# Four passes of an attention tile moved within their engines' order

## The chip, the cores and the metric

The kernel runs on one core of a Trainium2 chip, as one program. The metric is the device time of one execution in microseconds (us), shown as the median of several runs. The engines are TensorE (PE, with its weight loads as PEld), VectorE (DVE), ScalarE (ACT), GpSimd (POOL) and SyncE (SP), which here only issues DMAs. Each engine works through its own instructions in the order in which they are written; they meet at semaphores.

## The reference, cut to what matters

Four layers follow one another on x of 8 x 1024 x 256 in float32: an attention layer, an fp8 linear layer, a Mamba mixer with its MLP, and an int8 gated MLP. The change is in the first one alone:

```
q = (x @ Wq.T + bq);  k = (x @ Wk.T + bk);  v = (x @ Wv.T + bv)      # 16 heads of 16
logits = li[:, :, None, :] + lj[:, None, :, :] + rel_b               # 3 relations per pair of tokens
relation_probs = softmax(logits, axis=-1)
bias = einsum('bijk,hk->bhij', relation_probs, logical_bias)
gate = sigmoid(x @ gate_W.T + gate_b)
attn_weights = softmax(q k / scale + gate * bias, axis=-1)           # over j, for each head
out = einsum('bhij,bjhd->bihd', attn_weights, v) @ Wo.T + bo
```

x is layer-normed before it and added to the result.

## The kernel before

`attention` walks over 64 tiles of 128 rows of queries (8 batches of 8 tiles). The order of every engine is written out by hand: each has a function `body`, called once for each tile t, which loops over the 16 heads (`for u in range(H)`) and puts the other work of the tile between the heads by an `if` on u. `run` calls the bodies, the middle 48 tiles in a hardware loop. Flags say what a tile has: `look` (a next tile whose relation is prepared; 63 tiles), `pro` (projections for a tile one batch ahead; 56 tiles) and `post` (a previous tile to finish).

For head u of tile t the work runs through four engines:

- `pe_s`: TensorE makes the scores in `ps_s`, 128 x 1024 (L647). There is one such buffer, so head u+1 waits for DVE's `dve_s` of head u.
- `dve_f` (L491) on DVE writes rho * ps_p + R, the head's bias, into one of 8 row buffers (`srow`), for 12 heads. For the heads 1, 4, 8 and 12 (`POOL_HEADS`) `pool_f` does it on POOL in two passes, a multiplication (L408) and an addition (L410). `dve_f` of head u+1 stands ahead of `dve_s` of head u.
- `dve_s` (L502) on DVE takes the scores, adds the gated bias and finds the row's extremum (`nmax`), in one pass of 1024.
- `act_e` (L576) on ACT is the exponential in place; `pe_t` (L658) turns the row in eight blocks into `ps_t`, two heads later; `act_at` (L585) copies them out; `pe_pv` (L670) multiplies with V.

The relation of the next tile (64 x 128 x 1024 numbers each for three relations) is prepared in the same loop, by this chain:

- `dve_rel` step 0 (L474) on DVE: RT = max(Dj + a, 0), one tensor input and a scalar for each partition, both in SBUF. Step 1 (L477): a second maximum, with two tensor inputs in SBUF.
- `pool_rel` (L382), two passes on POOL, behind `pool_rem` (L372), which belongs to the projections and waits for `act_hi` (L542) on ACT.
- `act_rel` (L557, L561), three exponentials on ACT.
- `pool_sum` (L387, L391) on POOL.
- `act_y0` on ACT: a logarithm (step 0, L568), then an exponential of its negative (step 1, L571), which is the reciprocal of the sum.
- `pool_t` (L395) on POOL, `dve_y` (L482) on DVE, `pool_p` (L400) on POOL, and `act_p` (L537), which puts the probabilities into `ps_p` for the next tile's `dve_f`.

The other passes that the change or the prediction speaks of: `dve_v` (L455 and L459) adds V's bias from `ps_m`, which TensorE's `pe_v` filled (L635); `dve_xn` (L440) applies the layer norm of a later tile, one tensor input in SBUF; `act_o` (L589) copies the output of the tile before from `ps_o`, `pe_oT` (L680) turns it, and `dve_norm` (L508, L510) divides it; `pool_xrb` (L427) adds the output's bias. `ps_m` is one bank that the projections and the output of the tile before use in turn, under the semaphores `pm_free` and `om_free`.

POOL's order in a tile is: f of head 4, `pool_rem`, `pool_rel` twice, rstd, `pool_lo`, f of head 8, `pool_sum` twice, f of head 12, `pool_xrb`, `pool_t`, `pool_ge`, `pool_p` twice, `pool_gT`, f of the next tile's head 1, `pool_kappa`. The change doesn't touch it.

Of the kernel before, what the change touches and what calls it, by code (L numbers as in the profile page):

```python
# [34 lines left out]
def wait(eng, sem, value):  # L35

    if isinstance(value, int) and value <= 0:
        return
    eng.wait_ge(sem, value)
# [10 lines left out]
def attention(nc, x_in, wqk, wvg, bqk, rows, ident_in, parts_d, x_out):  # L50
# [13 lines left out]
    with ExitStack() as ctx:  # L64
# [365 lines left out]
        def dve_ln(dve, p, k):  # L430
            wait(dve, x_in_s, 16 * p + 16)
            nc.vector.bn_stats(stats[:], xt[:, k, :]).then_inc(ln_step, 1)
            alone(dve, ln_step, 3 * p + 1, dve_own)
            nc.vector.bn_aggr(mv[:], stats[:]).then_inc(ln_step, 1)
            dve.wait_ge(ln_step, 3 * p + 2)
            nc.vector.tensor_scalar(ve[:], mv[:, 1:2], LN_EPS, None, ALU.add).then_inc(ln_step, 1)
# [28 lines left out]
        def dve_rel(dve, t, k, slot, step):  # L465

            d10, d20 = (Dj[:, i, S * (slot // NT):S * (slot // NT) + S] for i in range(2))
            a10, a20 = (small[:, slot, H + i:H + i + 1] for i in range(2))
            if step == 0:
                wait(dve, kap_ok, t + 1)  # L470
                wait(dve, a12_ok, t + 1)
                wait(dve, p_ok, 2 * t)
                wait(dve, pm_free, 4 * (t - slot % NT + NT) - 1)
                nc.vector.tensor_scalar(RT[:], d10, a10, 0.0, ALU.add, ALU.max).then_inc(rel_step, 1)  # L474
            elif step == 1:
                dve.wait_ge(rel_step, 2 * t + 1)
                nc.vector.scalar_tensor_tensor(RT[:], d20, a20, RT[:], ALU.add, ALU.max).then_inc(rel_step, 1)  # L477
# [6 lines left out]
        def dve_f(dve, t, k, h):  # L484
            if h in POOL_HEADS:
                return
            r = rows_sb[h % NROW]
            if h == 0:
                wait(dve, pc_ok, t + 1)
            wait(dve, t_ok, 2 * (H * t + h) + 2)  # L490
            nc.vector.scalar_tensor_tensor(r[:], ps_p[:], rho[:, h:h + 1], R[k][0][:],  # L491
                                           ALU.mult, ALU.add).then_inc(fd_ok, 1)
# [61 lines left out]
        def act_rel(act, t, k, slot, step):  # L554
            if step == 0:
                wait(act, rel_step, 2 * t + 2)
                nc.scalar.activation(R[k][0][:], RT[:], ACT.Exp, scale=-1.0).then_inc(rel_exp, 1)  # L557
            else:
                wait(act, rel_d, 2 * t + step)
                dst = (R[k][1], R2)[step - 1]  # L560
                nc.scalar.activation(dst[:], dst[:], ACT.Exp,  # L561
                                     bias=small[:, slot, H + step - 1:H + step]).then_inc(rel_exp, 1)

        def act_y0(act, t, step):

            if step == 0:
                wait(act, rel_sum, 2 * t + 2)
                nc.scalar.activation(R2[:], RT[:], ACT.Ln).then_inc(rel_y0, 1)  # L568
            else:
                act.wait_ge(rel_y0, 2 * t + 1)  # L570
                nc.scalar.activation(R2[:], R2[:], ACT.Exp, scale=-1.0).then_inc(rel_y0, 1)  # L571

        def act_e(act, t, h):
            wait(act, s_ok, H * t + h + 1)
            r = rows_sb[h % NROW]
            nc.scalar.activation(r[:], r[:], ACT.Exp, scale=-1.0, bias=nmax[:, h % NROW:h % NROW + 1]  # L576
                                 ).then_inc(e_ok, 1)
# [9 lines left out]
        def act_o(act, o):  # L587
            wait(act, pv_ok, 2 + HG * (o + 1))
            nc.scalar.copy(O4[:], ps_o[:]).then_inc(o_ok, 1)  # L589
# [166 lines left out]
        def after(par, ib, n):  # L756

            return (par * NT + ib + n) % (2 * NT)
# [141 lines left out]
        def _(dve):  # L900
# [49 lines left out]
                dve_f(dve, 0, 0, 0)  # L950

            def body(dve, t, k, par, ib, pro, post, look, before):
                for u in range(H):
                    if u + 1 < H:
                        dve_f(dve, t, k, u + 1)
                    dve_s(dve, t, k, after(par, ib, 0), u)
                    if look and u < 2:
                        dve_rel(dve, t + 1, 1 - k, after(par, ib, 1), u)
                    if pro and u == 2:
                        dve_ln(dve, t + AHEAD, 1 - k)  # L960
                    if u == 3 and (not isinstance(t, int) or t >= 2):
                        dve_out(dve, t - 2)
                    if pro and u == 5:
                        dve_xn(dve, t + AHEAD, 1 - k)
                    if pro and u == 4:
                        dve_v(dve, t + NT, 1 - par, ib)
                    if post and u == 6:
                        dve_norm(dve, t - 1)
                    if look and u == 10:
                        dve_y(dve, t + 1)  # L970
                    if pro and u == 13:
                        dve_gate(dve, t + NT)
                    if pro and u == 14:
                        dve_qk(dve, t + AHEAD)
                    if look and u == 15:
                        dve_f(dve, t + 1, 1 - k, 0)
# [68 lines left out]
        @block.scalar  # L1045
        def _(act):
            def start(act):
                act.wait_ge(w_ready, 1)
                act_g_t(act, 0)
                act_xT(act, NT)  # L1050
                act_g_d(act, 0)
                act_g_e(act, 0)
                act_d(act, NT, NT)
                for s in range(2):
                    act_g_hi(act, 0, s)
                act_g_t(act, 1)
                for s in range(2):
                    act_g_mid(act, 0, s)
                act_g_ge(act, 0)
                act_g_d(act, 1)  # L1060
                act_g_e(act, 1)
                act_rel(act, 0, 0, 0, 0)
                act_rel(act, 0, 0, 0, 1)
                act_rel(act, 0, 0, 0, 2)
                for s in range(2):
                    act_g_hi(act, 1, s)
                for s in range(2):
                    act_g_mid(act, 1, s)
                for step in range(2):
                    act_y0(act, 0, step)  # L1070
                act_p(act, 0, 0)
                act_hi(act, NT)
                act_g_ge(act, 1)
                act_mid(act, NT)
                act.wait_ge(g_st, 16 * 8)

            def body(act, t, k, par, ib, pro, post, look, before):
                for u in range(H):
                    act_e(act, t, u)
                    if post and u == 5:  # L1080
                        act_o(act, t - 1)
                    if pro and u == 7:
                        act_xT(act, t + AHEAD)
                    if look and u in (7, 8):
                        act_y0(act, t + 1, u - 7)
                    if u >= LAG:
                        act_at(act, t, u - LAG)
                    elif post:
                        act_at(act, t - 1, H + u - LAG)
                    if u == 0 and (not isinstance(t, int) or t >= 2):  # L1090
                        act_aT(act, t - 2)
                    if followed(t, pro) and u == 0:
                        act_hi(act, t - 1 + AHEAD)
                    if followed(t, pro) and u == 2:
                        act_mid(act, t - 1 + AHEAD)
                    if look and u in (1, 3, 4):
                        act_rel(act, t + 1, 1 - k, after(par, ib, 1), (1, 3, 4).index(u))
                    if pro and u == 6:
                        act_gate(act, t + NT, 1 - par, ib)
                    if pro and u == 10:  # L1100
                        act_d(act, t + AHEAD, after(par, ib, AHEAD))
                    if look and u == 13:
                        act_p(act, t + 1, 1 - k)

            def finish(act):
                for u in range(H - LAG, H):
                    act_at(act, TILES - 1, u)
                act_aT(act, TILES - 2)
                act_o(act, TILES - 1)
                act_aT(act, TILES - 1)  # L1110

            act.preload_act_table_set("natural_log_exp_and_others")
            act.sem_inc(at_ok, 2)
            run(act, start, body, finish)

        @block.tensor
# [1296 lines left out]
```

## Time and profile before

| | us |
|---|---|
| median of 3 runs | 6053.53 (6041.44 to 6056.1) |
| the profiled execution, its own time | 6048.23 |
| its span | 6046.4 |
| attention, from 100 to 2830 us of the span | 2730.00, of which DVE is busy 2567.55, ACT 2623.23, PE 2409.03, POOL 2250.26 |

The span is the time between the first and the last instruction of the profiled execution. Busy times are sums over an engine's instructions. A tile's period is the distance between the starts of the same instruction in two tiles that follow one another. Durations overlap a little at their ends: the next instruction of DVE usually starts 0.08 us before the printed end of the one ahead.

### The profile page before, as it was taken

The numbers are of one execution on the slowest core, as the hardware profiler recorded it, in microseconds if no ns is written. First come the engines' busy times: TensorE is split into PE (matmuls) and PEld (weight loads), VectorE is DVE, ScalarE is ACT, GpSimd is POOL, SyncE is SP. The second block draws the span as 40 slices with busy tenths as digits, with TensorE's granted clock in tenths as the row PEclk, the third lists the DMA queues.
The fourth block names the chain that finished last, engine by engine and source line by source line (L and its number), as shares of the span: only waits on it lengthen the run. The fifth ranks groups of instructions, "written<-read, shape, count | busy, mean of one in ns | idle before, by whom it ended". The sixth has DMA issues, their size and how long they took to land. (4 is left out here: it accounts for less than half of the span.)

```text
span 6046.4 us, 122850 instructions
## 1 busy us (share of the span) xinstructions
PE 5371.3 (89%) x40162; PEld 3536.9 (58%) x40162; DVE 4703.6 (78%) x6099; ACT 4404.3 (73%) x7005; POOL 3700.2 (61%) x2010
## 2 busy tenths in 40 slices
PE   6888888888888898888799869999999979999999
PEld 4666666666666666655344345555555546666665
DVE  6999999999999999998898679999999942122221
ACT  4999999999999999999366678888888821111111
POOL 3888888888888888775100069999999930000000
PEclk8999999999999999999899889999999989999999
DMA  2121121212112121200355555565555531111110
GB/s 76 26 50 30 28 52 28 52 28 51 28 35 45 31 49 31 44 19 13 123 197 213 185 211 185 210 207 189 197 202 209 180 106 40 47 35 35 35 35 11
DMA packets 461360, 538.76 MB, mean 89 GB/s; under 512 B 237536, under 2 KB 337760, under 8 KB 460784
## 3 DMA queue, kind: packets, MB, share of 16 engines
q1 hardware_dynamic: 460784, 531.75, 28.1%
q8 instruction: 279, 4.57, 0.3%
q14 instruction: 297, 2.43, 0.1%
HBM read 370.31 MB, written 161.35 MB: 88 GB/s over the span
## 5 line engine op out<-in xcount | busy, mean ns | idle before, releaser
L502 DVE CUSTOM_DVE_ANT_0 srow<-srow,ps_s,small 128x1024 f32<-128x1024 f32 x1024 | 1305.0, 1274 | 71.6 <-issue 49.8
L576 ACT ACTIVATE srow<-srow,nmax 128x1024 f32<-128x1024 f32 x1024 | 1199.7, 1172 | 94.8 <-DVE nmax L502 83.0
L585 ACT COPY AT<-ps_t 128x512 f32<-128x512 f32 x2048 | 1110.6, 604 | 24.2 <-PE ps_t L658 23.4
L658 PEld LDWEIGHTS ps_t<-ident,srow 128*128 128x128 f32 x8192 | 959.2, 141 | 222.6 <-issue 16.8
L658 PE MATMUL ps_t<-ident,srow 128*128 128x128 f32 x8192 | 1077.1, 274 | 2.8 <-ACT AT L585 2.4
L1977 POOL TENSOR_TENSOR c_hc<-c_hs,c_cs 128x1024 f32<-128x1024 f32 x432 | 1010.1, 2365 | 63.9 <-DVE c_hs L2079 62.1
L491 DVE SCALAR_TENSOR_TENSOR srow<-ps_p,rho,R 128x1024 f32<-128x1024 f32 x768 | 976.0, 1271 | 0.0
L1938 PE MATMUL c_ps_y<-c_hc,c_ident 128*128 128x512 f32 x2048 | 945.9, 595 | 30.0 <-POOL c_hc L1977 17.1
L2079 DVE TENSOR_TENSOR_SCAN c_hs<-c_da,c_pd 128x1024 f32<-128x1024 f32 x384 | 859.8, 2274 | 58.0 <-PE c_pd L1929 54.6
L647 PE MATMUL ps_s<-K,Q 96*128 96x512 bf16 x2048 | 621.3, 385 | 286.8 <-DVE nmax L502 271.5
L2022 ACT ACTIVATE c_sT<-c_dxT,c_bT 128x256 f32<-128x256 f32 x1536 | 668.4, 494 | 105.7 <-PE c_pd L1929 95.7
L410 POOL TENSOR_TENSOR srow<-srow,R 128x1024 f32<-128x1024 f32 x256 | 608.1, 2376 | 46.9 <-POOL srow L408 46.9
L670 PE MATMUL ps_o<-AT,V 128*32 128x128 f32 x16384 | 609.6, 278 | 0.0
L2215 POOL TENSOR_TENSOR d_rstd<-d_ve,d_mhalf 128x4 f32<-128x4 f32 x16 | 16.3, 1017 | 899.1 <-DVE d_ve L1222 899.1
L1938 PEld LDWEIGHTS c_ps_y<-c_hc,c_ident 128*128 128x128 f32 x2048 | 359.9, 191 | 345.5 <-issue 304.7
L1929 PEld LDWEIGHTS c_pd<-c_ident,c_sT 128*128 128x128 f32 x3072 | 354.1, 142 | 343.0 <-issue 199.3
L1929 PE MATMUL c_pd<-c_ident,c_sT 128*128 128x128 f32 x3072 | 407.8, 276 | 109.5 <-DVE c_hc L2086 81.1
L670 PEld LDWEIGHTS ps_o<-AT,V 128*32 128x32 f32 x16384 | 402.9, 110 | 130.3 <-issue 128.6
L2013 ACT ACTIVATE c_da<-c_dt,c_a_neg 128x1024 f32<-128x1024 f32 x384 | 435.8, 1135 | 5.0 <-issue 5.0
L647 PEld LDWEIGHTS ps_s<-K,Q 96*128 96x128 bf16 x2048 | 141.6, 98 | 475.4 <-DVE nmax L502 420.9
L1970 POOL TENSOR_TENSOR c_db<-c_dx,c_bs 128x1024 f32<-128x1024 f32 x128 | 302.1, 2361 | 122.7 <-DMA c_bs<-bc_d 122.7
L2242 DVE TENSOR_TENSOR d_x<-d_ps_y,d_y 128x512 f32<-128x512 f32 x32 | 22.1, 692 | 438.6 <-PE d_ps_y L2317 438.6
(256 smaller groups left out, 8571.8 us busy)
## 6 DMA issues: line engine op xcount, KB each, us to landing
c_cs<-bc_d SPq DMA_DIRECT2D x256, 512.0 KB, 4.2
c_bs<-bc_d SPq DMA_DIRECT2D x64, 512.0 KB, 6.6
Q<-parts_d SPq DMA_DIRECT2D x384, 64.0 KB, 2.2
parts_d<-parts SPq DMA_DIRECT2D x57, 384.0 KB, 3.3
K<-parts_d SPq DMA_DIRECT2D x168, 128.0 KB, 4.3
sz_d<-b_sz SPq DMA_DIRECT2D x16, 1024.0 KB, 7.2
xv_d<-b_xv SPq DMA_DIRECT2D x16, 1024.0 KB, 7.9
dt_d<-b_ab SPq DMA_DIRECT2D x16, 1024.0 KB, 4.2
```

The source lines that it names most:

```text
L491: nc.vector.scalar_tensor_tensor(r[:], ps_p[:], rho[:, h:h + 1], R[k][0][:], ALU.mult, ALU.add).then_inc(fd_ok, 1)
L502: nc.vector.tensor_tensor_reduce(r[:], r[:], ps_s[:], small[:, slot, h:h + 1], BIG, ALU.add, ALU.min, nmax[:, h % NROW:h % NROW + 1]).then ...
L576: nc.scalar.activation(r[:], r[:], ACT.Exp, scale=-1.0, bias=nmax[:, h % NROW:h % NROW + 1]).then_inc(e_ok, 1)
L585: nc.scalar.copy(AT[h % NAT][:, HG * half:HG * half + HG, :], ps_t[:, half]).then_inc(at_ok, 1)
L647: last = nc.tensor.matmul(ps_s[:, n * 512:(n + 1) * 512], Q6[k][:, h, :], K6[:, h, n * 512:(n + 1) * 512], start=True, stop=True)
L658: last = nc.tensor.transpose(ps_t[:, half, i, :], rows_sb[h % NROW][:, j * P:(j + 1) * P], ident[:])
L670: last = nc.tensor.matmul(ps_o[32 * i:32 * i + 32, j, :], V[par][:, n, h, :], AT[h % NAT][:, n, :], start=(n == 0), stop=(n == NT - 1))
L1929: last = nc.tensor.transpose(pd[:, c, k * P:(k + 1) * P], src[:, k, c * P:(c + 1) * P], ident[:])
L1938: last = nc.tensor.matmul(ps_y[:, c, cut], ident[:], hc[place((n, c)) % NHC][:, cut], start=n == 0, stop=n == NS - 1)
L1977: nc.gpsimd.tensor_tensor(hc[place((n, c)) % NHC][:], hs[place((n, c)) % NHS][:], cs[n % NCS][:], ALU.mult).then_inc(hp_ok, 1)
L2022: last = nc.scalar.activation(sT[i % NSC][:, k, :], dxT[p][:, k, :], ACT.Copy, scale=bT[p][:, k, n:n + 1])
L2079: nc.vector.tensor_tensor_scan(h, gain, push, 0.0, ALU.mult, ALU.add).then_inc(h_ok, 1)
```

## The change

Four passes are written at other places. On DVE, `dve_rel` step 0 goes from behind `dve_s` of head 0 to the front of the tile, where it stands between `dve_f` of head 0 (which the body of the tile before issues last) and `dve_s` of head 0; and `dve_v` goes from behind `dve_s` of head 4 to behind `dve_xn`, which is behind `dve_s` of head 5. On ACT, `act_y0` step 1 goes from behind `act_e` of head 8 to ahead of it, and `act_o` from behind `act_e` of head 5 to ahead of it. No pass is added, removed or altered, and the orders of PE, POOL and SP stay.

```diff
@@ DVE's body @@
             def body(dve, t, k, par, ib, pro, post, look, before):
+                if look:
+                    dve_rel(dve, t + 1, 1 - k, after(par, ib, 1), 0)
                 for u in range(H):
                     if u + 1 < H:
                         dve_f(dve, t, k, u + 1)
                     dve_s(dve, t, k, after(par, ib, 0), u)
-                    if look and u < 2:
-                        dve_rel(dve, t + 1, 1 - k, after(par, ib, 1), u)
+                    if look and u == 1:
+                        dve_rel(dve, t + 1, 1 - k, after(par, ib, 1), 1)
                     if pro and u == 2:
                         dve_ln(dve, t + AHEAD, 1 - k)
                     if u == 3 and (not isinstance(t, int) or t >= 2):
                         dve_out(dve, t - 2)
                     if pro and u == 5:
                         dve_xn(dve, t + AHEAD, 1 - k)
-                    if pro and u == 4:
+                    if pro and u == 5:
                         dve_v(dve, t + NT, 1 - par, ib)
@@ ACT's body @@
                 for u in range(H):
+                    if look and u == 8:
+                        act_y0(act, t + 1, 1)
                     act_e(act, t, u)
-                    if post and u == 5:
-                        act_o(act, t - 1)
                     if pro and u == 7:
                         act_xT(act, t + AHEAD)
-                    if look and u in (7, 8):
-                        act_y0(act, t + 1, u - 7)
+                    if look and u == 7:
+                        act_y0(act, t + 1, 0)
                     if u >= LAG:
                         act_at(act, t, u - LAG)
...
                     if look and u in (1, 3, 4):
                         act_rel(act, t + 1, 1 - k, after(par, ib, 1), (1, 3, 4).index(u))
+                    if post and u == 4:
+                        act_o(act, t - 1)
```

What stands in DVE's order at the seam between two tiles (L447 and L449 finish the queries and keys of a tile ahead; the L491 is head 0's, the second L502 pair head 0's), before:

```order
140 L447 SCALAR_TENSOR_TENSOR qkf<-ps_m,b_qk,eT 128x128 x2
141 L449 TENSOR_TENSOR qkf<-ps_m,b_qk 128x256
142 L502 ISA srow,nmax<-srow,ps_s,small 128x1024
143 L502 ISA nmax 128x1
144 L491 SCALAR_TENSOR_TENSOR srow<-ps_p,rho,R_0 128x1024
145 L502 ISA srow,nmax<-srow,ps_s,small 128x1024
146 L502 ISA nmax 128x1
147 L474 TENSOR_SCALAR RT<-Dj,small 128x1024
148 L491 SCALAR_TENSOR_TENSOR srow<-ps_p,rho,R_0 128x1024
```

And now:

```order
140 L447 SCALAR_TENSOR_TENSOR qkf<-ps_m,b_qk,eT 128x128 x2
141 L449 TENSOR_TENSOR qkf<-ps_m,b_qk 128x256
142 L502 ISA srow,nmax<-srow,ps_s,small 128x1024
143 L502 ISA nmax 128x1
144 L491 SCALAR_TENSOR_TENSOR srow<-ps_p,rho,R_0 128x1024
145 L474 TENSOR_SCALAR RT<-Dj,small 128x1024
146 L502 ISA srow,nmax<-srow,ps_s,small 128x1024
147 L502 ISA nmax 128x1
148 L491 SCALAR_TENSOR_TENSOR srow<-ps_p,rho,R_0 128x1024
```

The relation pass L474 has moved one pass of L502 forward, to right behind head 0's L491.

DVE's order around heads 4 to 6 (the first L502 is head 4's), before:

```order
105 L502 ISA srow,nmax<-srow,ps_s,small 128x1024
106 L502 ISA nmax 128x1
107 L455 TENSOR_TENSOR V<-ps_m,row 128x16x16
108 L459 TENSOR_TENSOR zg<-ps_m,b_misc 128x18
109 L491 SCALAR_TENSOR_TENSOR srow<-ps_p,rho,R_0 128x1024
110 L502 ISA srow,nmax<-srow,ps_s,small 128x1024
111 L502 ISA nmax 128x1
112 L440 TENSOR_SCALAR xn<-xt,mv,rstd 128x256
113 L491 SCALAR_TENSOR_TENSOR srow<-ps_p,rho,R_0 128x1024
```

And now:

```order
105 L502 ISA srow,nmax<-srow,ps_s,small 128x1024
106 L502 ISA nmax 128x1
107 L491 SCALAR_TENSOR_TENSOR srow<-ps_p,rho,R_0 128x1024
108 L502 ISA srow,nmax<-srow,ps_s,small 128x1024
109 L502 ISA nmax 128x1
110 L440 TENSOR_SCALAR xn<-xt,mv,rstd 128x256
111 L455 TENSOR_TENSOR V<-ps_m,row 128x16x16
112 L459 TENSOR_TENSOR zg<-ps_m,b_misc 128x18
113 L491 SCALAR_TENSOR_TENSOR srow<-ps_p,rho,R_0 128x1024
```

V's two passes have moved from ahead of head 6's L491 to behind the layer norm's L440.

## Rows read from the trace of the kernel before

**Rows 1.** Busy time by stretch: start:end, length, then busy us of each engine

```profile
100.00:2830.00 2730.00, 2409.03 (x28884) 1803.76 (x28883) 2567.55 (x3700) 2623.23 (x3971) 2250.26 (x1342) 0.99 0.16 36
```

**Rows 2.** DVE's timeline, a tile's head: start, duration, engine, line, [idle before <-releaser]

```profile
1525.24 1.28 DVE L491 SCALAR_TENSOR_TENSOR srow<-ps_p,rho,R 128x1024 f32<-128x1024 f32 x1
1526.80 1.28 DVE L502 CUSTOM_DVE_ANT_0 srow<-srow,ps_s,small 128x1024 f32<-128x1024 f32 x1 [0.28 <-DVE srow L491]
...
1528.00 0.90 DVE L474 TENSOR_SCALAR RT<-Dj,small 128x1024 f32<-128x1024 f32 x1
1528.82 1.27 DVE L491 SCALAR_TENSOR_TENSOR srow<-ps_p,rho,R 128x1024 f32<-128x1024 f32 x1
...
1531.21 1.27 DVE L477 SCALAR_TENSOR_TENSOR RT<-Dj,small,RT 128x1024 f32<-128x1024 f32 x1
...
1568.39 1.28 DVE L491 SCALAR_TENSOR_TENSOR srow<-ps_p,rho,R 128x1024 f32<-128x1024 f32 x1
```

**Rows 3.** POOL's timeline, the same tile

```profile
1524.67 1.12 POOL L408 TENSOR_SCALAR srow<-R,rho 128x1024 f32<-128x1024 f32 x1 [0.55 <-PE ps_t L658]
1525.98 2.37 POOL L410 TENSOR_TENSOR srow<-srow,R 128x1024 f32<-128x1024 f32 x1 [0.18 <-POOL srow L408]
```

**Rows 4.** DVE's timeline, the kernel's first tile

```profile
89.54 1.54 DVE L474 TENSOR_SCALAR RT<-Dj,small 128x1024 f32<-128x1024 f32 x1
...
93.39 2.29 DVE L477 SCALAR_TENSOR_TENSOR RT<-Dj,small,RT 128x1024 f32<-128x1024 f32 x1
```

**Rows 5.** POOL's timeline, the kernel's first tile

```profile
88.18 2.35 POOL L410 TENSOR_TENSOR srow<-srow,R 128x1024 f32<-128x1024 f32 x1 [0.18 <-POOL srow L408]
90.50 1.56 POOL L408 TENSOR_SCALAR srow<-R,rho 128x1024 f32<-128x1024 f32 x1
92.24 2.36 POOL L410 TENSOR_TENSOR srow<-srow,R 128x1024 f32<-128x1024 f32 x1 [0.18 <-POOL srow L408]
```

**Rows 6.** Lines L474 and L440 over attention: duration ns min/median/max

```profile
L474 DVE TENSOR_SCALAR RT<-Dj,small x63: 817/899/1537, 89.5 to 2783.9; 128x1024 f32<-128x1024 f32 x63
...
L440 DVE TENSOR_SCALAR xn<-xt,mv,rstd x56: 409/567/2093, 107.7 to 2499.8; 128x256 f32<-128x256 f32 x56
```

**Rows 7.** POOL's timeline, the rest of that tile

```profile
1531.27 2.24 POOL L372 TENSOR_TENSOR qkf<-qkf,parts 128x512 f32<-128x512 f32 x1 [2.91 <-ACT parts L542]
...
1541.10 2.38 POOL L410 TENSOR_TENSOR srow<-srow,R 128x1024 f32<-128x1024 f32 x1 [0.18 <-POOL srow L408]
...
1552.22 0.75 POOL L427 TENSOR_TENSOR xr<-xr,row 128x256 f32<-128x256 f32 x1
1553.84 2.39 POOL L395 TENSOR_TENSOR RT<-RT,R 128x1024 f32<-128x1024 f32 x1 [0.87 <-ACT R L571]
```

**Rows 8.** DVE's timeline, behind head 4 to head 10 of that tile

```profile
1540.27 0.42 DVE L455 TENSOR_TENSOR V<-ps_m,row 128x256 f32<-128x256 f32 x1 [0.33 <-PE ps_m L635]
...
1540.69 1.27 DVE L491 SCALAR_TENSOR_TENSOR srow<-ps_p,rho,R 128x1024 f32<-128x1024 f32 x1
...
1543.08 0.56 DVE L440 TENSOR_SCALAR xn<-xt,mv,rstd 128x256 f32<-128x256 f32 x1
1543.56 1.27 DVE L491 SCALAR_TENSOR_TENSOR srow<-ps_p,rho,R 128x1024 f32<-128x1024 f32 x1
...
1556.26 1.23 DVE L482 SCALAR_TENSOR_TENSOR R<-RT,R 128x1024 f32<-128x1024 f32 x1 [0.46 <-POOL RT L395]
```

**Rows 9.** ACT's timeline, the reciprocal's exponential in that tile

```profile
1551.53 1.19 ACT L576 ACTIVATE srow<-srow,nmax 128x1024 f32<-128x1024 f32 x1
1552.58 1.08 ACT L571 ACTIVATE R<-R 128x1024 f32<-128x1024 f32 x1
```

**Rows 10.** TensorE's timeline, scores of head 12 of that tile

```profile
1558.74 0.60 PE L647 MATMUL ps_s<-K,Q 96*128 96x512 bf16 x2 [0.41 <-DVE nmax L502]
```

**Rows 11.** DVE's timeline, a tile of the last batch (no projections)

```profile
2675.61 0.26 DVE L508 RECIPROCAL rinv<-ps_m 128x16 f32<-128x16 f32 x1 [1.13 <-PE ps_m L680]
...
2685.38 1.23 DVE L482 SCALAR_TENSOR_TENSOR R<-RT,R 128x1024 f32<-128x1024 f32 x1 [0.67 <-POOL RT L395]
```

## The prediction

> **What bounds the kernel now.** I read the stretches first, since the change is in attention alone. From 100 to 2830 us of the span DVE is busy 2567.55 of 2730.00 us (94%) and ACT 2623.23 (96%) [rows 1]. Both are close to full, so a microsecond that DVE or ACT loses in a tile is a microsecond of the kernel unless a wait further on takes it up. Then I read the timelines of one tile in the middle, and follow its starts. Head 0's L491 starts at 1525.24 and that of the next tile at 1568.39, a period of 43.15 us [rows 2]. DVE's idle pieces in it are small, and each has a cause of its own: 0.28 us ahead of head 0's L502, which waits for the result of the L491 right ahead of it [rows 2]; 0.33 for TensorE ahead of V's bias, and 0.46 for POOL's L395 ahead of L482 [rows 8]. Taken one by one the moves aim at these.
>
> The third view decides, and it is POOL's timeline laid beside DVE's. L474 has one tensor input and 1024 columns, and is printed with 0.90 us, shorter than L491's 1.27 with as many columns. It starts at 1528.00 and ends at 1528.90 [rows 2]. POOL's addition for head 4 started at 1525.98 and ends at 1528.35 [rows 3], 0.55 ahead. In the first tile L474 starts at 89.54 and takes 1.54, to 91.08 [rows 4]; POOL's addition runs from 88.18 to 90.53 [rows 5], again 0.55 ahead. So L474's own work is 0.55 us, and the rest of its printed time is spent until POOL's pass is over: one starts 0.35 us ahead of POOL's end, the other 0.99, and both end 0.55 behind it. The same holds elsewhere: L440 starts at 1543.08 and ends at 1543.64 [rows 8], 0.16 behind the end of POOL's second pass for head 8 (1541.10 + 2.38 = 1543.48) [rows 7], and can take 0.41 or 2.09 [rows 6]; L477, with two inputs in SBUF, takes 1.27 alone [rows 2], but 2.29, to 95.68, when it comes into a POOL pass that ends at 94.60 [rows 4, 5]. It goes the other way too. POOL's L408 takes 1.12 [rows 3] but 1.56 where L474 holds on until 91.08 [rows 4, 5], and L372, half as wide as the passes of 2.38, takes 2.24, because L477 runs until 1532.48 [rows 2, 7]. These passes of DVE and those of POOL exclude one another. L491 and L502, which take one input from PSUM, run through POOL's passes at their usual length [rows 2, 3].
>
> The Trainium skill says this in SBUF — State Buffer, section "SBUF: two separate sides": VectorE and GpSimd share a pair of ports, whoever starts first holds it for its whole instruction, and the other is blocked. It counts VectorE's two-port modes and instructions with two SBUF inputs among the holders. By that rule the relation pass can't be put into GpSimd's addition at its printed price, which speaks against this change; the sum by the rule is the one below.
>
> **The change part by part.** All numbers are shifts of starts against the tile above.
>
> *The relation pass at the front.* Head 0's L491 starts at 1525.24 and lasts 1.28; the next instruction of DVE can start 0.08 ahead of its end, at 1526.44. There L474 now stands. POOL's addition has held on since 1525.98 and does until 1528.35 [rows 3], so L474 ends at 1528.90, as it did before, after 2.46 us in place of 0.90. Head 0's L502 then starts at 1528.82 in place of 1526.80, and head 2's L491 one pass of L502 (1.20) later, at 1530.02 in place of 1528.82 [rows 2]: +1.20 us. The 0.28 us of idle time is gone, and is counted in this. Without the exclusion L474 would give the place at once and everything from here would come 0.36 earlier.
>
> What could hide the 1.20? Queued behind L474 on DVE are all heads. ACT has e of head 0 later by 2.02, but catches up over its pieces of waiting by head 2. POOL's next pass, L372, waits for ACT's L542 and after that ends about 1.03 behind L477 [rows 2, 7]. L477 comes 1.20 later, L372 ends 1.20 later, and all of POOL's line up to head 8 with it.
>
> *V's bias behind the layer norm.* V's two passes take 0.42 from 1540.27 to 1540.69, and the wait ahead of them is 0.33, or 0.41 counted from start to start [rows 8]. Both leave this place: 1.20 - 0.83 = +0.37 when L440 comes up, at 1543.45. But POOL's pass for head 8 now ends at 1543.48 + 1.20 = 1544.68 [rows 7], and L440 0.16 behind it, at 1544.84. What V's passes filled before is now spent inside L440. They follow from 1544.76, and head 7's L491 starts at 1545.18 in place of 1543.56 [rows 8]: +1.62. TensorE's `pe_oT` waits for V in `pm_free`, and head 7's scores stand behind it; but these wait for head 6's L502, which follows head 7's L491 and so V itself by over 1.2 us. V's later place costs TensorE nothing.
>
> *The output copy ahead of head 5's exponential.* ACT does the same work; the exponential of head 5 comes one copy later, and its row is transposed two heads further on. DVE's `dve_norm` stands behind head 6, and head 7's scores wait for head 6 anyway. Nothing here; it is worth something only in the last batch, below.
>
> *The reciprocal's exponential ahead of head 8's.* L571 stood one exponential later than it will, 1552.58 against 1551.53 [rows 9], and POOL's L395 waited 0.87 for it [rows 7]. POOL is free for L395 at 1552.22 + 0.75 = 1552.97 before, 1554.17 now. ACT's exponential of head 6 waits for DVE, so ACT is as late as DVE here, about 1.65: L571 starts at 1551.53 + 1.65 and ends at about 1554.3, and L395 at 1556.7. L482 comes up on DVE at 1556.26 - 0.54 + 1.62 = 1557.34 [rows 8], and waits no more. The 0.54 (0.46 of idle and 0.08 of overlap) are given back: +1.08.
>
> *Behind it.* TensorE had 0.41 us of room ahead of head 12's scores [rows 10]; it is 1.62 late against DVE's 1.08, so 0.13 of the difference stays. The tile ends between +1.08 and +1.21; I take +1.2. POOL's first pass for head 4 waits for TensorE's transposes of head 12 [rows 3] and is as late as DVE is, so the next tile meets the same addition at the same place.
>
> *Tiles.* 56 tiles have projections. In the first of them L474 would come at about 88.0, ahead of the addition at 88.18 [rows 5], and is spared. 55 x 1.2 = 66 us. In the 7 further tiles with a relation pass but no projections the +1.20 meets a wait of 1.13 for `pe_oT` [rows 11], which the earlier output copy takes away, and 0.67 for L395; I count 0. Bounds for each of the 55: without V's loss in L440, +1.20 - 0.83 + 0.42 = +0.79 ahead of L482, and +0.3 to +0.4 behind it; with no wait given back at L482, +1.62.
>
> **The sum.** 6048.23 + 66 = 6114 for the profiled execution. Its time lies 5.3 us below the median of 6053.53, whose runs span 15 us, so the median would be 6120; I take the middle, 6117. Under 0.3% (18 us) this kernel's measurement doesn't tell from no change.
>
> **The rivals.**
> *L474 gets in first* (ends on the other side). If it comes up before 1525.98, it takes 0.55 and POOL's addition waits, as L408 did in the first tile. Then head 0's L502 starts at 1526.96, head 2's L491 0.66 early, L477 and POOL too. L440 keeps DVE back until 0.16 behind the head 8 pass, V's 0.42 follow, -0.24; L482 waits for nothing, -0.78; TensorE's line gives about -0.65. 55 x -0.65 = -36: 6015. Speaks for it: the margin is only 0.46 (1526.44 against 1525.98). Against: the addition is tied to head 12's transposes, these to the same scores as DVE's passes, and to reverse the order takes the whole margin in every tile. Chance 0.08.
> *No exclusion at the new place at all*, whatever makes L474 end 0.55 behind POOL now: L474 would cost 0.82, head 2 would come 0.36 early, and POOL's chain from L542 to L395 would let the tile gain 0.44: 55 x -0.44 = -24, 6027. Sixty-three of sixty-three starts speak against it in that none is shorter than 0.817 us. Chance 0.03.
> *V isn't caught in L440*: only the lower bound, 55 x 0.35 = 19, 6070. It needs POOL's head 8 pass to be less late than DVE. POOL sits idle 2.91 us ahead of L372 [rows 7], which speaks for it; that L477 now and then decides when L372 can work speaks against. Chance 0.13.
> *ACT or TensorE falls behind for good*, so that the wait at L482 isn't given back: 55 x 1.62 = 89, 6140. ACT at 96% speaks for it. Chance 0.10.
> *Nothing moves the end*, as DVE's loss meets slack that I don't see: 6050. Chance 0.03.
> The forecast itself (6100 to 6133) has 0.63.
>
> **How the numbers follow.** The time is the forecast's. The range leaves out both gains and no change (0.14) and reaches from the lower to the upper bound: 6066 to 6142. Faster by over 0.3%: 0.11. Slower by over 0.3%: the forecast, the upper case and most of the lower one, 0.84. The rest, 0.05.
>
> **What would show it.** In the changed kernel's trace L474 should take about 2.4 us nearly everywhere and end 0.55 behind a POOL L410; L440 should take about 1.4; V's wait for TensorE and that of L482 for L395 should be gone; ACT should wait about 2 us for head 0's `nmax`; the period should be 44.3. L474 at 0.55 to 0.9 us would prove me wrong, and so would L440 at 0.57 with a period near 43.5.

## The result, and the profile after

The changed kernel takes 6134.04 us (median of 4 runs, 6126.8 to 6151.94) against 6054.32 before: a ratio of 1.0146, 95% interval 1.0129 to 1.0163. By the ratio that is some 88 us slower; the two medians are 80 us apart. Some executions were disturbed (a granted clock of 0.37 to 0.93, three of e8's six among them), and every number here is of undisturbed ones.

The profiled execution took 6132.81 us, 85 more than the one before, and nearly all of that is in attention. From the first L477 to the last it was 2694 us and is 2777, by DVE's timelines (93.39 to 2787.46 before, 94.16 to 2871.61 after).

DVE's timeline of a tile in the middle, to be laid beside [rows 2] and [rows 8] (start, duration, engine, line):

```profile
1714.44 1.28 DVE L491 SCALAR_TENSOR_TENSOR srow<-ps_p,rho,R 128x1024 f32<-128x1024 f32 x1
1715.64 2.46 DVE L474 TENSOR_SCALAR RT<-Dj,small 128x1024 f32<-128x1024 f32 x1
1718.02 1.27 DVE L502 CUSTOM_DVE_ANT_0 srow<-srow,ps_s,small 128x1024 f32<-128x1024 f32 x1
...
1721.61 1.27 DVE L477 SCALAR_TENSOR_TENSOR RT<-Dj,small,RT 128x1024 f32<-128x1024 f32 x1
...
1732.64 1.40 DVE L440 TENSOR_SCALAR xn<-xt,mv,rstd 128x256 f32<-128x256 f32 x1
1733.96 0.41 DVE L455 TENSOR_TENSOR V<-ps_m,row 128x256 f32<-128x256 f32 x1
...
1746.54 1.22 DVE L482 SCALAR_TENSOR_TENSOR R<-RT,R 128x1024 f32<-128x1024 f32 x1
...
1758.72 1.28 DVE L491 SCALAR_TENSOR_TENSOR srow<-ps_p,rho,R 128x1024 f32<-128x1024 f32 x1
```

POOL's timeline of the same tile, to be laid beside [rows 3, 7]:

```profile
1715.18 2.37 POOL L410 TENSOR_TENSOR srow<-srow,R 128x1024 f32<-128x1024 f32 x1 [0.18 <-POOL srow L408]
1722.47 1.44 POOL L372 TENSOR_TENSOR qkf<-qkf,parts 128x512 f32<-128x512 f32 x1 [4.93 <-ACT parts L542]
...
1731.51 2.38 POOL L410 TENSOR_TENSOR srow<-srow,R 128x1024 f32<-128x1024 f32 x1 [0.18 <-POOL srow L408]
...
1743.62 2.38 POOL L395 TENSOR_TENSOR RT<-RT,R 128x1024 f32<-128x1024 f32 x1 [0.28 <-ACT R L571]
```

L474 comes up at 1715.64, 0.46 us into POOL's addition, which ends at 1717.55; L474 ends 0.55 later, at 1718.10. L440 ends at 1734.04, 0.15 behind POOL's pass for head 8 (1733.89). The waits ahead of V's L455 and ahead of L482 are gone. From L491 to L491 it is 44.28 us, against 43.15.

In the first tile the two meet in the other order. L474 starts at 89.75 and takes 0.74, to 90.49; POOL's addition starts 0.14 behind it and takes 2.80 in place of 2.37:

```profile
89.89 2.80 POOL L410 TENSOR_TENSOR srow<-srow,R 128x1024 f32<-128x1024 f32 x1 [0.18 <-POOL srow L408]
```

The lines L474 and L440 over the whole of attention (ns, min/median/max):

```profile
L474 DVE TENSOR_SCALAR RT<-Dj,small x63: 737/2454/2722, 89.7 to 2865.2; 128x1024 f32<-128x1024 f32 x63
...
L440 DVE TENSOR_SCALAR xn<-xt,mv,rstd x56: 1327/1416/2183, 107.3 to 2576.5; 128x256 f32<-128x256 f32 x56
```

Two tiles by stretch (start:end, length, busy us of PE, PEld, DVE, ACT and POOL, then TensorE's granted clock as a share of full speed, the DMA engines' busy share and GB/s):

```profile
1721.61:1765.89 44.28, 38.40 (x474) 29.07 (x464) 43.03 (x61) 41.71 (x65) 35.70 (x22) 1.00 0.12 29
1541.66:1587.68 46.02, 41.66 (x456) 31.30 (x448) 43.22 (x63) 41.34 (x64) 35.59 (x22) 0.91 0.19 38
```

The first is what was forecast. The second was not: 46.02 us at a mean granted clock of 0.91. Of the 62 periods from L477 to L477, 18 take more than 45 us, against 6 before. TensorE's timeline in the second tile:

```profile
1539.40 0.60 PE L647 MATMUL ps_s<-K,Q 96*128 96x512 bf16 x2 [2.57 <-DVE nmax L502]
...
1555.86 0.63 PE L680 MATMUL ps_m<-ident,O 128*128 128x128 f32 x4 [1.07 <-ACT O L589]
1557.03 0.60 PE L647 MATMUL ps_s<-K,Q 96*128 96x512 bf16 x2 [0.55 <-DVE nmax L502]
1557.48 1.76 PE L658 MATMUL ps_t<-ident,srow 128*128 128x128 f32 x8
1559.17 1.51 PE L670 MATMUL ps_o<-AT,V 128*32 128x128 f32 x24
...
1561.51 1.04 PE L658 MATMUL ps_t<-ident,srow 128*128 128x128 f32 x8
```

The same tile's stretches around its two waits, in the columns of the windows above:

```profile
1538.00:1540.50 2.50, 1.10 (x8) 0.91 (x9) 2.50 (x5) 1.12 (x2) 0.00 (x0) 1.00 1.00 152
1540.50:1544.00 3.50, 3.50 (x40) 2.22 (x39) 3.50 (x5) 2.99 (x6) 1.35 (x2) 0.51 1.24 166
1557.50:1561.00 3.50, 3.50 (x35) 2.70 (x34) 2.59 (x4) 3.36 (x7) 2.97 (x3) 0.52 0.02 7
```

TensorE waits 2.57 us for head 0's `nmax`, then runs a stretch at 0.51, which is the lower of its two levels, 1.2 GHz. It waits again ahead of the turned output (1.07) and of head 7's scores (0.55), and again runs at half: eight transposes take 1.76 us instead of 1.04, and 24 products 1.51 instead of the 0.86 of the tile at full clock. The DMA engines move much in the first of the two slow stretches (a busy share printed as 1.24) and next to nothing in the second (0.02), so DMA traffic isn't what they share. Head 8's scores come late, and DVE has 1.53 us of idle time ahead of its L502 of head 8, where the tile at full clock has none:

```profile
1561.85 1.28 DVE L502 CUSTOM_DVE_ANT_0 srow<-srow,ps_s,small 128x1024 f32<-128x1024 f32 x1 [1.53 <-issue]
```

The Trainium skill, TensorE: Matmul & The Clock Gate, Part 1, says that a monitor sets this clock by how busy the engine has been recently; the rows agree in that both drops stand behind waits.

### The profile page after: what moved, and what is told of

Its sections match the earlier page's. It is cut to its first block and busy times, and to the rows that moved or that the text cites. A ratio compares the mean times of both kernels' runs of the same rounds, so it can differ in the third digit from the quotient of the medians.

```text
span 6131.0 us, 122850 instructions
## 1 busy us (share of the span) xinstructions
PE 5412.3 (88%) x40162; PEld 3566.3 (58%) x40162; DVE 4823.9 (79%) x6099; ACT 4390.8 (72%) x7005; POOL 3658.4 (60%) x2010
## 5 line engine op out<-in xcount | busy, mean ns | idle before, releaser
L502 DVE CUSTOM_DVE_ANT_0 srow<-srow,ps_s,small 128x1024 f32<-128x1024 f32 x1024 | 1304.1, 1274 | 90.6 <-issue 66.4
L658 PEld LDWEIGHTS ps_t<-ident,srow 128*128 128x128 f32 x8192 | 974.8, 143 | 250.3 <-ACT AT L585 34.7
L658 PE MATMUL ps_t<-ident,srow 128*128 128x128 f32 x8192 | 1098.0, 278 | 13.1 <-ACT AT L585 12.7
L491 DVE SCALAR_TENSOR_TENSOR srow<-ps_p,rho,R 128x1024 f32<-128x1024 f32 x768 | 975.5, 1270 | 0.0
L647 PE MATMUL ps_s<-K,Q 96*128 96x512 bf16 x2048 | 633.6, 391 | 329.1 <-DVE nmax L502 313.6
L670 PE MATMUL ps_o<-AT,V 128*32 128x128 f32 x16384 | 628.3, 284 | 0.0
L670 PEld LDWEIGHTS ps_o<-AT,V 128*32 128x32 f32 x16384 | 415.2, 112 | 136.3 <-issue 133.7
```

Source lines behind the costliest of these rows:

```text
L502: nc.vector.tensor_tensor_reduce(r[:], r[:], ps_s[:], small[:, slot, h:h + 1], BIG, ALU.add, ALU.min, nmax[:, h % NROW:h % NROW + 1]).then ...
L647: last = nc.tensor.matmul(ps_s[:, n * 512:(n + 1) * 512], Q6[k][:, h, :], K6[:, h, n * 512:(n + 1) * 512], start=True, stop=True)
L658: last = nc.tensor.transpose(ps_t[:, half, i, :], rows_sb[h % NROW][:, j * P:(j + 1) * P], ident[:])
L670: last = nc.tensor.matmul(ps_o[32 * i:32 * i + 32, j, :], V[par][:, n, h, :], AT[h % NAT][:, n, :], start=(n == 0), stop=(n == NT - 1))
```

## The experiments

Ratios, and the times given with a sign, are to the kernel before, run on the same chip in turn. The periods are the distances between the starts of `dve_rel`'s step 1 in DVE's timeline, 62 of them. The period "at full clock" is the median of those whose granted clock stays at 1.00; "below full clock" are those with a lower mean.

### One part of the change at a time

e1, the relation pass alone (a diff against before):

```diff
+                if look:
+                    dve_rel(dve, t + 1, 1 - k, after(par, ib, 1), 0)
                 for u in range(H):
...
-                    if look and u < 2:
-                        dve_rel(dve, t + 1, 1 - k, after(par, ib, 1), u)
+                    if look and u == 1:
+                        dve_rel(dve, t + 1, 1 - k, after(par, ib, 1), 1)
```

> The first relation pass alone moved to the tile's front; V and the two ACT passes where they were. Exclusion theory (a DVE pass of L474's kind waits until POOL's running pass is over): L474 takes about 2.45 us and ends 0.55 behind POOL's addition for head 4, head 2 comes 1.20 late, and since POOL's whole line follows L477, the wait ahead of L482 stays: period about 44.3 us, and the time about as much above before as the whole change (+65 to +90 us). Rival theory (the price is V's pass caught behind L440, and L474 is cheap because the 0.28 us of idle time ahead of it goes): period 43.15 or less, time within 20 us of before.

Measured: 1.0163 (1.0139 to 1.0187), +98 us, more than the whole change and more than the +65 to +90 expected. L474 has a median of 2453 ns. At full clock the period is 44.35; other tiles take 45.3 and 46.8. The exclusion theory holds for the tile, and the rival falls. The excess lies in the 35 periods below full clock; e10 tests whether the clock makes it.

e2, V's bias alone:

```diff
-                    if pro and u == 4:
+                    if pro and u == 5:
                         dve_v(dve, t + NT, 1 - par, ib)
```

> V's bias alone moved behind the layer norm's L440. Exclusion theory: V's wait of 0.33 us goes, L440 comes 0.83 us earlier but still ends 0.16 us behind POOL's pass for head 8, so it takes about 1.4 us, head 7 comes 0.42 late, and the wait ahead of L482 shrinks from 0.46 to about 0 in exchange: period 43.15, time within 10 us of before. Rival theory (the waits of DVE are independent prices): the 0.33 us is gained in each of 55 tiles, -18 us. Second rival (V behind L440 is the change's price): +20 us or more.

Measured: 1.0100 (1.0080 to 1.0120), +60 us. That is in the range of the second rival, +20 us or more, and V behind L440 does have a price: the period at full clock is 43.56, not 43.15. But 0.41 us in 56 tiles are only 23 us. The rest lies in the 38 periods below full clock, most of them of 44.6 to 44.9 us. DVE's timeline of a tile at full clock:

```profile
1222.24 1.39 DVE L440 TENSOR_SCALAR xn<-xt,mv,rstd 128x256 f32<-128x256 f32 x1
1223.55 0.41 DVE L455 TENSOR_TENSOR V<-ps_m,row 128x256 f32<-128x256 f32 x1
...
1227.29 1.28 DVE L502 CUSTOM_DVE_ANT_0 srow<-srow,ps_s,small 128x1024 f32<-128x1024 f32 x1 [0.22 <-PE ps_s L647]
...
1236.66 1.23 DVE L482 SCALAR_TENSOR_TENSOR R<-RT,R 128x1024 f32<-128x1024 f32 x1 [0.45 <-POOL RT L395]
```

L440 takes 1.39 as expected, but the wait ahead of L482 is still 0.45. ACT's exponential of head 6 waits for DVE (0.28 us), so the reciprocal and with it L395 come as late as DVE does, and the 0.42 of V's passes can't go into that wait.

TensorE shows the other half. Its waits ahead of head 6's scores and of the turned output, first in the kernel before (the tile of [rows 8]), then in e2's tile above, where the second line is the wait ahead of head 7's scores:

```profile
1543.22 0.61 PE L647 MATMUL ps_s<-K,Q 96*128 96x512 bf16 x2 [0.67 <-DVE nmax L502]
1545.48 0.63 PE L680 MATMUL ps_m<-ident,O 128*128 128x128 f32 x4 [0.78 <-ACT O L589]
```

```profile
1225.47 0.63 PE L680 MATMUL ps_m<-ident,O 128*128 128x128 f32 x4 [1.52 <-ACT O L589]
1226.49 0.60 PE L647 MATMUL ps_s<-K,Q 96*128 96x512 bf16 x2 [0.39 <-DVE nmax L502]
```

With V out of the way head 6's scores no longer wait, but the turned output comes no earlier. Two waits of 0.67 and 0.78 us have become one of 1.52 and one of 0.39.

e3, the two ACT passes alone, which is the second half of the change's diff:

```diff
+                    if look and u == 8:
+                        act_y0(act, t + 1, 1)
                     act_e(act, t, u)
-                    if post and u == 5:
-                        act_o(act, t - 1)
...
+                    if post and u == 4:
+                        act_o(act, t - 1)
```

> The two ACT passes alone moved (output copy ahead of head 5's exponential, reciprocal's exponential ahead of head 8's), DVE as before. My working: POOL's L395 starts 0.87 us earlier, the wait of 0.46 ahead of L482 goes, TensorE's line limits the gain to about 0.41 us a tile: period 42.7, time -20 to -28 us. Rival (ACT is at 96% and its order doesn't matter, the wait comes back as another): period 43.1, time within 8 us of before.

Measured: 0.9960 (0.9944 to 0.9977), -24 us, with a period of 42.67. Both are as worked out.

e4, all but the relation pass: e2's and e3's diffs together.

> The whole change without the first relation pass: V's bias and both ACT passes moved. Exclusion theory: V's pass behind L440 costs 0.42 us, the earlier L395 gives back 0.54: period 43.0 to 43.15, time -10 to 0 us against before; so the relation pass alone makes the change's loss. Rival (V behind L440 is the price): +20 us or more.

Measured: 1.0059 (1.0041 to 1.0076), +36 us. At full clock the period is 43.08, inside what was expected. The time is not: -10 to 0 us was expected, and +36 is in the rival's range. 38 of the 62 periods are below full clock, many of them of 44.6 us. Against e3 the V move costs 0.41 us a tile at full clock and about 60 us in all.

At full clock the three parts add up: 1.20 for the relation pass (e1), 0.41 for V (e2) and -0.48 for ACT's passes (e3) make 1.13 us a tile, and the change has 1.14. The whole times don't: 98 + 60 - 24 = 134 us, and the change has 88.

### The exclusion, from both sides

e5, POOL's addition for head 4 left out (head 4's bias lacks the term R, and the semaphore is counted up at once):

```diff
-            nc.gpsimd.tensor_tensor(r[:], r[:], R[k][0][:], ALU.add).then_inc(fp_ok, 1)
+            if h == 4:
+                pool.sem_inc(fp_ok, 1)
+            else:
+                nc.gpsimd.tensor_tensor(r[:], r[:], R[k][0][:], ALU.add).then_inc(fp_ok, 1)
```

> The whole change, and POOL's addition for head 4 (the second of its two passes, the one that runs while the relation pass comes up) left out, so that head 4's bias lacks one term; its semaphore is counted up at once. Exclusion theory: L474 takes 0.55 us at the new place instead of 2.45, head 2 comes about 0.66 us early, and the period of a tile in which TensorE's clock stays up is 42.5 us. Rival theory (L474 is slow at its new place because of what stands next to it on DVE or because of its operands): it stays at 2.4 us, the period at 44.3. The stalls of TensorE ahead of the turned output stay, so some tiles still lose about 1.5 us to the lower clock: time -36 to +5 us against before.

Measured: 0.9944 (0.9929 to 0.9958), -34 us. The moved pass, which is L477 in this kernel, over all of attention (ns, min/median/max):

```profile
L477 DVE TENSOR_SCALAR RT<-Dj,small x63: 737/743/754, 89.6 to 2759.5; 128x1024 f32<-128x1024 f32 x63
```

The instruction, its operands and its place are those of the change; only POOL's pass is gone, and 2454 ns become 743. The period at full clock is 42.59, against 42.5 expected. The pass's own work is 0.74 us, not 0.55.

e6, the maximum taken with a tensor in PSUM in place of zero (from the second tile on, so another result):

```diff
-                nc.vector.tensor_scalar(RT[:], d10, a10, 0.0, ALU.add, ALU.max).then_inc(rel_step, 1)
+                if isinstance(t, int) and t == 0:
+                    nc.vector.tensor_scalar(RT[:], d10, a10, 0.0, ALU.add, ALU.max).then_inc(rel_step, 1)
+                else:
+                    nc.vector.scalar_tensor_tensor(RT[:], d10, a10, ps_p[:], ALU.add, ALU.max).then_inc(rel_step, 1)
```

> The whole change, but the moved relation pass takes the maximum with ps_p, a tensor in PSUM, in place of zero (one input in SBUF, one in PSUM, as L491; it computes something else from the second tile on). Exclusion theory: like L491 it runs through POOL's passes and takes 1.27 us at the new place, about 1.1 us less than in the change though it needs more than twice the 0.55 us for itself; period at full clock about 43.05 us, as with all but the relation pass moved, time +25 to +45 us against before. Rival theory (the pass is slow at the front of the tile whatever it reads): 2.4 us again, period 44.3.

Measured: 1.0054 (1.0040 to 1.0069), +33 us. DVE's timeline, then POOL's, in this kernel:

```profile
1511.62 1.27 DVE L477 SCALAR_TENSOR_TENSOR RT<-Dj,small,ps_p 128x1024 f32<-128x1024 f32 x1
1512.81 1.28 DVE L505 CUSTOM_DVE_ANT_0 srow<-srow,ps_s,small 128x1024 f32<-128x1024 f32 x1
```

```profile
1511.17 2.38 POOL L410 TENSOR_TENSOR srow<-srow,R 128x1024 f32<-128x1024 f32 x1 [0.18 <-POOL srow L408]
```

It comes up 0.45 us into POOL's addition, as in the change, and ends 0.66 us before it, after 1.27 us. An instruction that needs 0.74 us alone was made one that needs 1.27, and a tile at full clock became 1.2 us shorter (43.1). So the place alone doesn't make the pass slow; it is slow there only while it reads and writes SBUF alone and POOL works beside it. The operation has changed as well, from TENSOR_SCALAR to SCALAR_TENSOR_TENSOR, but that isn't what frees it: L477 is of that operation too, with two inputs in SBUF, and took 2.29 us in a POOL pass [rows 4]. The time is in the range expected, though 45 of e6's 62 periods are below full clock.

### The clock

e7, the whole change, with TensorE kept at work in its two waits by transposes made again into the same place:

```diff
                 wait(pe, at_ok, 2 * U + half + 1)
-                for i in range(HG):
+                for i in tuple(range(HG)) * (3 if half and h == 3 else 1):
...
-            for c in range(DC):
+            for c in tuple(range(DC)) * 5:
                 last = nc.tensor.transpose(ps_m[:, c * P:(c + 1) * P], attn[:, c * P:(c + 1) * P], ident[:])
```

> The whole change, with TensorE kept at work in its two longest waits: the two transposes of the output at the end of a tile are made 5 times, and the last four of head 3's eight transposes 3 times, each time with the same result into the same place. Clock theory: of the 83 us that attention lost, some 20 are tiles of 46.0 us in place of 44.3, in which TensorE ran at 1.2 GHz for 3 to 7 us after these waits; with the fill the clock stays at 2.4 GHz, no tile takes 46, and the time is +62 to +70 us against before, 15 to 25 under the change. Rival theory (these tiles wait for something else, as a DMA or an instruction load): they stay, and the fill adds to the time.

Measured: 6103.13 us, 1.0082 (1.0067 to 1.0096), +50 us, so 31 to 39 less than the change (by medians, by ratios). TensorE does 16 transposes more in a tile and the kernel is faster. From 100 to 2740 us, in the changed kernel, then with the fill:

```profile
100.00:2740.00 2640.00, 2304.58 (x27170) 1730.96 (x27172) 2531.03 (x3503) 2452.82 (x3747) 2085.49 (x1278) 0.98 0.17 36
```

```profile
100.00:2740.00 2640.00, 2370.52 (x28378) 1820.88 (x28378) 2549.22 (x3535) 2475.73 (x3782) 2111.83 (x1290) 1.00 0.17 36
```

The period is 44.29 in nearly every tile; where the change had six of about 46.0 in a row there is none, and 10 periods are below full clock in place of 28. It came out 12 us below the lower end of what I had expected. The table at the end of this section fits that: the kernel before has 23 us above its period at full clock, this one 11, so the fill takes away 12 us that the change hadn't brought. What the fill would do in the kernel before wasn't tried.

e9, e2 with the fill in head 3's transposes alone:

> V's bias alone moved, as in e2, and the last four of head 3's transposes made 3 times, so that TensorE works in its wait of about 1.5 us ahead of the turned output. Clock theory: of e2's +60 us some 38 are tiles at the lower clock (44.6 us in place of 43.55); with the fill all tiles take 43.55 and the time is +15 to +28 us against before. Rival theory (the longer tiles come from V's place itself): +55 us or more.

Measured: 1.0027 (1.0016 to 1.0039), +16 us against e2's +60. The period is 43.57 in nearly all tiles, and 8 are below full clock in place of 38. V's place costs 0.42 us a tile by itself; the 44 us between e2 and e9 are the clock's, by the only edit between them and the periods that it takes away.

e10, e1 with both fills:

> The relation pass alone moved, as in e1, with TensorE filled at both places as in e7. Clock theory: tiles of 44.3 us throughout, time +45 to +65 us against before, where e1 had +98. Rival theory (e1's tiles of 45.3 and 46.8 us come from ACT's order, which e1 has as before, and not from the clock): they stay, +90 us or more.

Measured: 1.0108 (1.0091 to 1.0125), +65 us against e1's +98, the upper end of what was expected. The period is 44.35. But for a few where one batch ends and the next begins, the tiles of 45.3 and 46.8 are gone, so they came from the clock, and the relation pass alone costs about as much a tile as the whole change.

### A version that beats both

e8, e3 with the relation pass one pass later than before, behind head 2's L491:

```diff
+                    if look and u == 1:
+                        dve_rel(dve, t + 1, 1 - k, after(par, ib, 1), 0)
                     dve_s(dve, t, k, after(par, ib, 0), u)
-                    if look and u < 2:
-                        dve_rel(dve, t + 1, 1 - k, after(par, ib, 1), u)
+                    if look and u == 1:
+                        dve_rel(dve, t + 1, 1 - k, after(par, ib, 1), 1)
```

> A version for speed: both ACT passes moved as in the change, V where it was, and the relation pass one pass later than before, behind head 2's L491, where POOL has just ended its addition and idles. Exclusion theory: L474 takes 0.55 us in place of 0.90, head 2's scores and with them all of POOL's line come 0.35 us earlier, on top of the 0.41 to 0.48 us of the ACT passes: period 42.3 to 42.4 us, time -40 to -50 us. Rival theory (DVE's wait elsewhere takes the 0.35 up): period 42.67 as with the ACT passes alone, -21 us.

Measured: 0.9902 (0.9885 to 0.9919), -59 us (three runs, 5994.38 to 5996.54), more than the -40 to -50 expected. The pass over all tiles:

```profile
L474 DVE TENSOR_SCALAR RT<-Dj,small x63: 740/744/1448, 90.1 to 2729.5; 128x1024 f32<-128x1024 f32 x63
```

It no longer meets POOL, the period is 42.53, and 6 periods are below full clock. 42.53 against 42.67 is a gain of 0.14 in the middle tiles, not the 0.35 that I had expected, for the pass takes 0.74 alone and not 0.55. That makes 8 us. Most of the rest of the gain over e3, some 24 us by the table, lies in tiles that e3 has at 44 to 46.7 us and this kernel hasn't. This was not foreseen, and why e8 has fewer of them than e3 wasn't tried.

### All runs side by side

From the profiled executions, but for the last column. The third number is what the first 56 periods take beyond 56 times the period at full clock; before and in the versions alike some of it lies where one batch of tiles ends and the next begins.

| kernel | period at full clock, us | periods below full clock | first 56 periods, us above 56 times the period at full clock | time against before, us |
|---|---|---|---|---|
| before | 43.15 | 10 | 23 | |
| the change | 44.29 | 28 | 36 | +88 |
| e1, relation pass alone | 44.35 | 35 | 52 | +98 |
| e2, V's bias alone | 43.56 | 38 | 59 | +60 |
| e3, ACT's two passes alone | 42.67 | 12 | 36 | -24 |
| e4, all but the relation pass | 43.08 | 38 | 82 | +36 |
| e5, change without POOL's addition | 42.59 | 23 | 42 | -34 |
| e6, change with a PSUM input | 43.12 | 45 | 74 | +33 |
| e7, change with TensorE filled | 44.29 | 10 | 11 | +50 |
| e8, the faster version | 42.53 | 6 | 12 | -59 |
| e9, e2 with TensorE filled | 43.57 | 8 | 19 | +16 |
| e10, e1 with TensorE filled | 44.35 | 11 | 13 | +65 |

## Why the prediction was right and where it was wrong

**The exclusion: right, and shown.** L474 takes 2.45 us (forecast about 2.4), L440 1.40 (about 1.4), the tile 44.28 (44.3), and the first tile is spared (its L474 takes 0.74). e5 takes away POOL's pass and e6 an input in SBUF beside it, and either ends the wait. The rivals that L474 gets in first or that nothing excludes it are out.

**The price of 0.55 for L474 itself: mis-sized.** Alone it takes 0.74 (e5, e8). 0.55 is what is left behind the end of POOL's pass; the first 0.19 runs while it waits. It doesn't touch the forecast, since the pass waited in all tiles but the first, but it made e8's gain in the middle tiles smaller than expected.

**The relation pass at +1.20, V at +0.42 behind L440, the wait at L482 given back: right for the change.** The periods of e1, 44.35, and of e4, 43.08, bear out the parts. For V alone the last step didn't hold (e2): the wait ahead of L482 shrinks only with the earlier reciprocal, which the ACT passes bring.

**The sum, 55 x 1.2 = 66 us: right for what it holds, and a term is missing.** At full clock the loss is 44.29 - 43.15 = 1.14 us a tile, 63 us for 55 tiles. Measured are 80 us by the medians and 88 by the ratio. In the profiled executions attention grew by 83: 56 periods at 1.14 or 1.15 us make 64, the first 56 periods hold 13 more beyond that (36 us against 23 in the table), and the last six 6.

**The step that failed: "V's later place costs TensorE nothing".** With it failed the silence on TensorE behind "ACT has e of head 0 later by 2.02". Both said rightly that no scores are late because of TensorE's order. But both moves lengthen single waits of TensorE: 2.57 us at the tile's head where it was 0.56 to 0.71, and in the change's tile at full clock 1.44 ahead of head 7's scores, where there was none (its row is below). In some tiles the granted clock falls to half in or behind such a wait, and DVE then waits for TensorE. V's move alone brings 28 more periods below full clock and 37 us beyond its 23 (e2), and filling the wait takes 44 us back (e9); the relation pass alone is the same case (e1, e10). In the change together the term that the sum put at nothing is some 17 to 25 us, what is left of 80 to 88 when 63 are taken off. The 31 to 39 us that e7's fill saves are more than that, since the fill also takes away drops that the kernel before had. Why the moves together bring fewer drops than either alone stays open.

```profile
1736.90 0.60 PE L647 MATMUL ps_s<-K,Q 96*128 96x512 bf16 x2 [1.44 <-DVE nmax L502]
```

**The range and the rivals.** The measured median, 6134, lies in the range of 6066 to 6142, near its upper end; the ratio makes 6142.7 of 6054.32, just above it. The bounds held only terms of DVE and POOL. The rival "ACT or TensorE falls behind for good" gave +89 us, close to the 88, but by another way: it wanted the wait ahead of L482 not given back, and that wait is gone in the changed tile. Its number was met by luck.

**The output copy "nothing here": unsettled.** The two ACT passes were never moved apart, so no run shows what the copy alone does. Adding both to V's move changed nothing in the number of periods below full clock (38 in e2 and in e4), and the time beyond the period at full clock is no smaller (59 and 82 us).

**The last batch, 0 us: right within 2 us at full clock.** Its last six periods sum to 261.4 us after and 255.1 before, +6 us. In e7 they are 256.3, so some 5 of the 6 are the clock's. In e10, which has the relation pass moved but not ACT's passes, they are 262.5: the pass costs 1.2 us a tile there too, and the earlier ACT passes take most of it back, as was worked out.

## What to carry to other kernels

Lay POOL's timeline beside DVE's before a pass is moved. A pass whose end keeps the same distance to the end of a POOL pass, whatever its start, is one that POOL excludes; here these were the TENSOR_SCALAR passes on SBUF (L474, L440) and the one with two inputs in SBUF (L477). Such a pass takes its own time only where POOL pauses, so look for the pause and put it there (e8). And look at the length of TensorE's single waits before and after a move, even where nobody waits for TensorE: redundant transposes in them made the changed kernel faster.

## What the runs showed of the hardware that was not expected

- TensorE's clock: the same wait of 2.57 us ahead of head 1's scores was followed by a stretch at 0.51 in one tile (from 1540.5 us) and by none in another, which stayed at 1.00. Rows of the second one, in the windows' columns:

```profile
1717.00:1721.00 4.00, 1.65 (x18) 1.29 (x22) 4.00 (x5) 1.93 (x4) 0.54 (x1) 1.00 0.06 11
```

What decides between the two stays open here; that work in the waits prevents most of the drops is shown by e7, e9 and e10.
- A DVE pass that waits for POOL seems to get through its first 0.19 us while it waits. That is read from two durations of L474: 0.74 alone, 0.55 behind POOL's end.
- Not every DVE pass with one f32 input in SBUF is excluded. In the tile of [rows 2] the statistics pass L432 comes up inside a POOL pass, takes 0.42 us (0.41 to 0.43 in all 57 of the kernel before), and ends before POOL's pass does (two passes of POOL are merged in its line):

```profile
1534.80 0.42 DVE L432 BATCH_NORM_STATS2 stats<-xt 128x6 f32<-128x256 f32 x1
```

```profile
1533.47 4.70 POOL L382 TENSOR_TENSOR R<-Dj,RT 128x1024 f32<-128x1024 f32 x2
```

- POOL's L372 takes 1.44 us after the change and 2.24 before [rows 7]. L477 now ends 0.41 us behind its start instead of 1.21, and L372 ends 1.03 us behind L477 in both: the exclusion lengthens POOL's passes as printed, too.
